# Decoder recurrence: a gapless table of shifted alignments, its second copy issued by ScalarE, and the state's product taken out from behind the alignment

## The reference, cut to what matters

```python
def step(carry, tgt):
    s, c, alpha = carry
    f = lax.conv_general_dilated(alpha, conv_w, (1,), 'SAME', ...)       # 10 filters of 101 taps over the last alignment
    e = jnp.einsum('a,bta->bt', va, jnp.tanh(enc_proj + (s @ Wa_s.T)[:, None, :] + jnp.einsum('bft,af->bta', f, Wa_f) + ba))
    e = jnp.where(mask, e, jnp.float32(-1e+30))
    alpha_new = jax.nn.softmax(e, axis=1)[:, None, :]
    g = jnp.einsum('bt,btd->bd', alpha_new[:, 0], hbatch)
    y = ...
    rec = tgt @ L_ys.T + s @ L_ss.T + g @ L_gs_w.T + L_gs_b
    ig, fg, cg, og = jnp.split(rec, 4, axis=1)
    c_next = _sig(fg) * c + _sig(ig) * jnp.tanh(cg)
    s_next = _sig(og) * jnp.tanh(c_next)
```

## Time and profile before

| | us |
|---|---|
| median of 3 runs | 4106.64 (4104.02 to 4106.89) |
| the profiled execution | 4107.34 |
| its span, first to last instruction | 4105.6 |
| the recurrence in it, about | 2200 to 3608 |

### The profile page before, as it was taken

One profiled execution on the slowest core, in us unless ns is written; L12 is line 12 of the kernel. 1 busy time (PEld: TensorE's weight loads), 2 busy tenths in 40 slices (PEclk: granted clock), 3 DMA queues, 4 the chain that ended last, 5 costly groups with the idle time before them and its releaser, 6 DMA issues. The chain is left out here.

```text
span 4105.6 us, 117583 instructions
## 1 busy us (share of the span) xinstructions
PE 3312.4 (81%) x47218; PEld 2204.7 (54%) x47218; DVE 2217.7 (54%) x5373; ACT 1602.2 (39%) x3966; POOL 502.7 (12%) x1854
## 2 busy tenths in 40 slices
PE   7556568544489999998697999999999999965998
PEld 4424145222276776665345666666666666633554
DVE  2655757588845555555203555555555555563444
ACT  2221144344422222222113666666666666622222
POOL 0000411233200000000000000000000000033222
PEclk9576689776799999999898999999999999976888
DMA  2000020200010000000111222222222222201000
GB/s 94 3 3 0 10 45 9 85 0 0 0 44 0 0 0 0 0 0 1 51 34 39 53 50 53 53 51 52 53 53 50 53 52 51 53 17 51 22 26 31
DMA packets 185328, 127.18 MB, mean 31 GB/s; under 512 B 18448, under 2 KB 174433, under 8 KB 185201
## 3 DMA queue, kind: packets, MB, share of 16 engines
q1 hardware_dynamic: 182512, 123.17, 11.2%
q0 software_dynamic: 2752, 3.18, 0.5%
HBM read 115.57 MB, written 13.90 MB: 32 GB/s over the span
## 5 line engine op out<-in xcount | busy, mean ns | idle before, releaser
L1834 PE MATMUL ps<-de_hg,st_at 128*32 128x128 f32 x16384 | 519.6, 276 | 0.3 <-DVE st_at L2000 0.3
L1834 PEld LDWEIGHTS ps<-de_hg,st_at 128*32 128x32 f32 x16384 | 427.1, 110 | 31.8 <-DVE st_at L2000 0.5
L1900 ACT ACTIVATE st_th<-ps,st_sw 128x128 f32<-128x128 f32 x1024 | 292.0, 368 | 253.5 <-PE ps L1806 253.5
L1980 DVE TENSOR_TENSOR st_th<-ps,st_sw 128x512 f32<-128x512 f32 x256 | 177.1, 692 | 125.3 <-PE ps L1806 125.3
L1247 PEld LDWEIGHTS ps<-sa_xt,w_wq 128*128 128x128 f32 x2048 | 234.7, 194 | 11.0 <-issue 9.2
L1769 POOL COPY de_ah<-st_at 128x8 f32 (+1 forms) x256 | 50.6, 198 | 1551.5 <-DVE st_at L2000 1551.5
L1247 PE MATMUL ps<-sa_xt,w_wq 128*128 128x128 f32 x2048 | 237.9, 278 | 1.9 <-ACT sa_xt L1363 1.9
L1318 PE MATMUL ps<-sa_wo,sa_ct 128*128 128x512 f32 x512 | 225.0, 598 | 13.2 <-issue 13.2
L1794 PE MATMUL ps<-st_hk,st_cwt 64*32 64x128 f32 x8192 | 171.8, 274 | 73.9 <-DMA st_hk<-padded_alignments 68.4
L2241 PE MATMUL ps<-rf_wb,rf_sp 128*128 128x512 bf16 x768 | 212.6, 444 | 0.9 <-DVEq L2361 0.9
L1806 PE MATMUL ps<-st_fs,st_waf 32*128 32x128 f32 x4096 | 186.6, 296 | 5.7 <-ACT st_fs L1890 1.7
(11 more groups left out here) (410 smaller groups left out, 6483.6 us busy)
## 6 DMA issues: line engine op xcount, KB each, us to landing
st_hk<-padded_alignments SPq DMA_DIRECT2D x508, 129.0 KB, 3.1
X<-in_x_dram SPq DMA_DIRECT2D x16, 512.0 KB, 9.1
out_dram<-X SPq DMA_DIRECT2D x16, 512.0 KB, 2.7
w_wq<-in_Wq_perm_dram SPq DMA_DIRECT2D x1, 4096.0 KB
sa_wo<-in_Wo_perm_dram SPq DMA_DIRECT2D x1, 4096.0 KB, 14.2
gate_inputs<-dp_ro SPq DMA_DIRECT2D x16, 256.0 KB, 2.3
st_rin<-gate_inputs SPq DMA_DIRECT2D x128, 32.0 KB, 2.4
rf_wf<-in_weightT_dram SPq DMA_DIRECT2D x8, 512.0 KB, 3.7
```

Of the source, the lines that this page charges most:

```text
L1834: ins = pe.matmul(R[g][32 * q:32 * q + 32, :], at[g][:, b, :], hg[:, BG * g + b, q * P:(q + 1) * P], start=False, stop=(b == BG - 1), tile ...
L1900: ins = act.activation(th[g][:, b, :], sums(g, 0)[:, b // 2, (b % 2) * P:(b % 2 + 1) * P], ACT.Tanh, bias=sw[g][:, b:b + 1])
L1980: dve.tensor_tensor(th[g][:, 4:8, :].rearrange("p (k s) n -> p k s n", s=2), sums(g, 1).rearrange("p k (s n) -> p k s n", s=2), sw[g][:, 4 ...
```

## The change

The tile loses its gap: pitch 129 in place of 132. SP issues only the first copy of the windows; the second is issued from ACT's queue by the new function `copy_shifted`, which waits for `ex_out` as SP does and stands in ACT's list between keep_filters and squash. On PE the wait for `al_ready` goes from the head of the half into `turn_alignment`, behind `state_term`; in its place at the head stands a wait for `exp_done` of group `g`, since the state's product of group `o` goes into the PSUM bank from which the exponential of group `g` is taken.

```diff
-            hk = pair("hk", [P, BG // 2, P + 4])
+            hk = pair("hk", [P, BG // 2, P + 1])
...
                         sp.wait_ge(ex_out[o], 16 * m + 16)
-                        for r in range(2):
-                            sp.dma_start(hk[o][64 * r:64 * r + 64, :, 0:P + 1], hankel(o, r)).then_inc(hk_in[o], 16)
+                        sp.dma_start(hk[o][0:64, :, :], hankel(o, 0)).then_inc(hk_in[o], 16)
...
                     def turn_alignment(g, n):
+                        pe.wait_ge(al_ready[g], n + 1)
                         pe.transpose(AT[g], al[g][:, :], ident[:, :]).then_inc(at_ps[g], 1)
 
                     def half(g, n, o, m, u, more):
                         front = not isinstance(m, int) or m <= LAST
-                        pe.wait_ge(al_ready[g], n + 1)
                         if front:
+                            pe.wait_ge(exp_done[g], n + 1)
                             state_term(o, m)
                         turn_alignment(g, n)
...
+                    def copy_shifted(g, n):
+                        act.wait_ge(ex_out[g], 16 * n + 16)
+                        act.dma_start(hk[g][64:128, :, :], hankel(g, 1)).then_inc(hk_in[g], 16)
+
...
                         if front:
                             keep_filters(o, m)
+                        if more:
+                            copy_shifted(g, n)
+                        if front:
                             squash(o, m)
                         if more:
                             fill(g, n + 1)
```

## The result

The changed kernel takes 4133.66 us (median of 4 runs, 4129.14 to 4137.34) against 4106.77 for the kernel before (4 runs). The ratio is 1.007, with a 95% interval of 1.0058 to 1.0083: slower, by 27 us. The forecast was 4135.

A forecast was written before the change was run, and what follows sets the result against it. Waits in the recurrence, not clock or bandwidth, bound it at 5.51 us a half; the new ACT loop, 4.93 + 0.61 + 0.08 = 5.62, adds 254 x 0.11 = 28 us to 4106.6: 4135, range 4115 to 4165.

The forecast's parts named there:

- The bound before: Ahead of PE's filter products the second copy lands last, by about 0.2 us; landing earlier gains 0.12 us a half.
- The loop: On ACT, squash to next copy issue 4.93 us, plus issue and restart: 5.62 us a half against 5.51.
- X: Length of the added DMA issue on ACT, taken from SP's issue of the same transfer: 0.61 us, bounds 0.33 and 1.24.
- the restart: On ACT, from the end of the issue to the start of the squash: 0.08 us.
- rival 1: ACT's issue is short: at 0.33 us the run takes 4064 us, shorter still 4043; chance 30%.
- The state's product: On PE, run ahead of the alignment wait, it lets the transposition follow the alignment directly: gain 0.13 us.
- the early landing: The second copy, issued 0.6 us earlier, lands at about 3007.9, before the gates.
- a filter product that still waits for the DMA: Sign of being wrong, on PE: it would mean two queues don't land earlier than one.
- the squash still put down to PE's product: Sign of being wrong, on ACT: the profile still names PE's L1806 as the squash's releaser.
- The rival with the lock of the Trainium skill: SP's and ACT's issues wait for each other: 4295 us if ACT is second, 4214 with half of it; chance 16%.

The follow-up runs named there:

- e7: The second copy left out (its half of the windows stays zero, so the result is wrong), on top of e2: 4047.33 us, ratio 0.9869.
- e3: Against the kernel before, only the second copy moved to ScalarE's queue; pitch 132, alignment wait as before: 4134.27 us, ratio 1.0075.
- e5: ScalarE issues both copies of the windows and SP none, on top of e2: 4293.86 us, ratio 1.047.
- e11: On top of e2, ScalarE issues a small unused load that waits for the padded rows' landing; SP issues both copies: 4101.97 us, ratio 1.0006.
- e12: Both copies move two of their four rows, on top of e2 and e3; part of the computation is left out: 4141.23 us in one run.
- e2: Against the kernel before, only the alignment wait moved behind the state's product: 4097.88 us, ratio 0.9985.
- e9: On top of e2, ScalarE issues a small unused load without waiting for the padded rows' landing; SP issues both copies: 4100.48 us, ratio 0.9989.

## Why the prediction was right, point by point

- **The bound before.** The second copy is the last to come before the filter products in most halves (199 waits): shown by e7, where the wait vanished and 50 us with it. The gain was mis-sized: 0.12 us was read from one half, in which the filter products start 3.63 us behind SP's issue and wait for no DMA. The mean between 2300 and 3400 is 3.81, and in e7 3.39, so they could come 0.4 us earlier.
- **The loop.** 4.93 + 0.61 + 0.08 = 5.62 us forecast; 4.94 + 0.60 + 0.10 = 5.64 in the half above, 5.63 as the mean. e3, e5 and e11 set X to 0.60, 1.25 and 0.36, and the loop gives the time of the first two within 4 us; in the third it is only now and then the longest path. e12 shows that the period stays at 5.63 when the windows no longer matter. That the forecast meets the median within 2 us is closer than its terms: the issue was put 0.01 too long and the restart 0.02 too short, and the four runs spread over 8 us.
- **X from SP's rows.** ScalarE's issue of the same transfer costs what SP's does: 0.597 against 0.601. The small load costs 0.334, like the contiguous rows on SP. The guess that the contiguous tile might make X short (rival 1) fell: 0.597 with the gapless tile and with pitch 132.
- **The state's product.** The prediction saw 0.13 us of gain on PE and asked whether ACT can use it; e2 without the issue gained 6 us by the ratio over 254 halves, 0.02, and in the changed kernel the loop leaves none.
- **A step that failed: the early landing.** The prediction let the second copy land 3.1 us behind ScalarE's issue, about 3007.9, 0.6 us earlier than before. Its median landing was 3.7 us behind it, as late as SP's second did (0.6 + 3.1). It had no effect on the sum, because the loop was longer anyway (e12), but without it the whole intent of the change is missing: even a free issue on ScalarE would have left the windows where they were. The prediction had named the sign of this, a filter product that still waits for the DMA, and it showed in 103 halves.
- **A sign against it that came and misled:** the squash still put down to PE's product was listed as a sign of being wrong. The changed kernel's rows do put it down to L1805, though ScalarE starts it 0.12 to 0.47 us behind DVE and 0.10 behind its own issue. The sign was badly chosen; the distance to DVE is the better one.

The rival with the lock of the Trainium skill ("Perfetto Trace Analysis", section "DMA Instruction — HWDGE (DVE, Sync)"): the page lets the wait for the descriptor generator show in the issue's own duration. Here both issues start at 3002.41 and both last 0.60 us, as SP's does where it is the only one (0.601 in e7), so no such wait shows in them. In e11 the small load starts 0.06 us behind SP's first copy, lasts 0.35 and is over while SP still issues; apart from SP's, in e9, it lasts 0.334. The second copy's landing 0.6 us late could come from a request that waits behind the sequencer; that fits its late first packet, but is only argued.

The best version measured, with all of the computation in it, is e2_state, the state's product without the other two parts: 4097.88 us.

## What to carry to other kernels

An engine that issues a DMA starts nothing that stands behind it in its list until the issue is over (0.60 us here, and 0.10 to the next instruction), so ask at which moment it issues and not how idle it is: ScalarE had a hole of 0.9 to 1.1 us in each half, but the landing that it had to wait for fell into its middle. Write down the loop that the new wait closes and add the issue: it tells the size, the sign, and the length of issue from which it turns. A releaser in a profile row can be the wrong one: compare with another engine that waits for the same semaphore. And test the prize first by leaving the transfer out (e7), then whether the second queue brings it; here the prize was up to 50 us and the queue brought none of it.

## What the runs showed of the hardware that I had not expected

- Two copies asked for at the same moment from two queues land 3.0 and 3.6 us later (e3); one behind the other from one queue they land at 3.0 each (e5), and 0.6 + 3.0 is the same moment. A second queue saved SP's issue and nothing of the landing. SP's load of the gate inputs, issued behind the copy, also took longer to land, counted from its own issue: a median of 3.1 us in the changed kernel, 2.4 before.
- The length of an issue goes with the kind of transfer on ScalarE as on SP (0.334 and 0.597), and not with its number of rows (0.596 with half of them).
- In e9 the issue ran beside ScalarE's own computing instruction (the kept filters at 3000.19 for 0.47 us, the issue at 3000.20 for 0.33; again at 3005.44 and 3005.52): there the instruction in the works didn't hold up the issue behind it.
